# Turning the next batch's tokens by crossbar transfers instead of TensorE, with two V tiles moved between the last contexts

## The reference

```
xn = layernorm(x)
q, k, v = heads(xn @ Wq.T), heads(xn @ Wk.T), heads(xn @ Wv.T)     # 16 heads of 32
q, k = rope(q), rope(k)
s = softmax(causal(q @ k.T / sqrt(32))) @ v, heads joined, @ Wo.T
h = gelu(bitlinear(xn, w_fc))          # 512 -> 2048; bitlinear: layer norm, ternary weights
g = silu(bitlinear(h, w_proj))         # 2048 -> 512
out = x + s * g
```

## Time and profile before

| | us |
|---|---|
| time, median of 3 runs | 1127.14 (1125.05 to 1127.7) |
| the profiled execution's own time | 1127.08 |
| its span in the trace | 1125.4 |
| TensorE busy | 1100.0 (98%) |
| VectorE busy | 843.7 (75%) |
| ScalarE busy | 791.3 (70%) |
| GpSimd busy | 503.7 (45%) |

### The profile page before, as it was taken

How to read it: one execution, slowest core, us unless ns; L and a number is a source line. 1 busy time by engine, 2 the same in 40 slices (tenths; PEclk the granted TensorE clock), 3 DMA queues, 4 the chain that set the end, 5 groups by cost and what they waited for, 6 DMA issues and landing times.

```text
span 1125.4 us, 20210 instructions
## 1 busy us (share of the span) xinstructions
PE 1100.0 (98%) x7548; PEld 609.2 (54%) x7548; DVE 843.7 (75%) x1595; ACT 791.3 (70%) x1510; POOL 503.7 (45%) x915
## 2 busy tenths in 40 slices
PE   4989999999999999999999999999999999999998
PEld 3555654458444574446644475445844467444663
DVE  7987977798558986489756996479865898648964
ACT  4788984589835888269872798448982588826984
POOL 2135361473606635265433745156361663526533
PEclk9999999999999999999999999999999999999999
DMA  9492002920019101381016510193011910136101
GB/s 317 160 106 47 1 3 66 110 79 21 2 39 158 40 2 31 43 127 38 3 29 74 95 38 4 29 105 83 20 7 40 153 38 2 31 47 85 39 16 62
DMA packets 52610, 67.30 MB, mean 60 GB/s; under 512 B 9376, under 2 KB 34336, under 8 KB 52000
## 3 DMA queue, kind: packets, MB, share of 16 engines
q1 hardware_dynamic: 52512, 66.02, 32.3%
HBM read 31.98 MB, written 8.40 MB: 36 GB/s over the span
## 4 chain that ended last, share of the span: by engine, by line
PE 92%; DVE 3%; ACT 2%; POOL 1%; DMA 1%; issue 1%; SPq 0%; DVEq 0%; POOLq 0%
PE banks L433 23%; PE banks L561 20%; PE banks L606 14%; PE banks L687 7%; PE banks L668 7%; PE banks L540 6%; PE banks L450 5%; PE banks L617 4%; PE banks L547 2%; ACT banks L873 2%; PE banks L464 1%; PE banks L404 1%; PE banks L471 1%; DVE mix L1163 1%; DMA v_sb<-in_L_attn_Wv_dram 1%
## 5 line engine op out<-in xcount | busy, mean ns | idle before, releaser
L873 ACT ACTIVATE banks<-banks,mix,scl 128x384 f32<-128x384 f32 (+2 forms) x384 | 248.1, 649 | 21.1 <-POOL mix L1375 15.7
L1163 DVE TENSOR_REDUCE mix<-banks 128x1 f32<-128x512 f32 (+3 forms) x352 | 216.1, 638 | 27.6 <-PE banks L547 23.3
L561 PE MATMUL banks<-xT,fcT 128*128 128x512 f16 x1024 | 229.4, 381 | 3.2 <-ACT xh_buf L837 2.7
L606 PE MATMUL banks<-proj_ones,arena 128*128 128x256 f16 (+1 forms) x1536 | 213.3, 273 | 0.0
L896 ACT ACTIVATE arena<-banks,scl 128x1280 f32<-128x1280 f32 x128 | 162.1, 1329 | 30.8 <-PE banks L668 27.9
L1366 POOL TENSOR_TENSOR xh_buf<-xh_buf 128x512 f32<-128x512 f32 x120 | 152.3, 1269 | 70.4 <-ACT xh_buf L837 69.2
L433 PE MATMUL banks<-xT,qkT 128*128 128x512 f16 x768 | 168.5, 379 | 0.0
L561 PEld LDWEIGHTS banks<-xT,fcT 128*128 128x128 f16 x1024 | 98.8, 98 | 123.1 <-ACT xh_buf L837 6.7
L606 PEld LDWEIGHTS banks<-proj_ones,arena 128*128 128x128 f16 x1536 | 141.7, 97 | 35.8
L1375 POOL TENSOR_SCALAR mix<-mix,scl 128x1 f32<-128x1 f32 (+1 forms) x288 | 76.5, 266 | 174.3 <-DVE mix L1163 172.9
L1135 DVE TENSOR_TENSOR arena<-banks,mix 128x512 f32<-128x512 f32 x128 | 79.5, 684 | 93.9 <-PE banks L433 93.9
(11 more groups left out here) (165 smaller groups left out, 1445.0 us busy)
## 6 DMA issues: line engine op xcount, KB each, us to landing
stacks<-xh_buf SPq DMA_DIRECT2D x96, 128.0 KB, 5.2
stacks<-split_buf SPq DMA_DIRECT2D x96, 128.0 KB, 7.1
out_dram<-arena SPq DMA_DIRECT2D x32, 256.0 KB, 2.0
xr_buf<-in_L_attn_x_dram SPq DMA_DIRECT2D x7, 1024.0 KB, 9.9
resid<-in_L_attn_x_dram SPq DMA_DIRECT2D x28, 256.0 KB, 5.7
stacks<-in_L_ffn_w_fc_dram SPq DMA_DIRECT2D x1, 4096.0 KB, 26.1
arena<-in_L_ffn_w_proj_dram SPq DMA_DIRECT2D x1, 4096.0 KB, 15.1
mix<-norm_row SPq DMA_DIRECT2D x8, 256.0 KB, 5.0
```

Of the source, the lines that this page charges most:

```text
L561: mm = pe.matmul(banks[:, UP_BANKS[f % NUB], :], fcT[:, c, f * P:(f + 1) * P], xT[:, part, c, :], start=(c == 0 and part == 0), stop=(c == ...
L606: mm = pe.matmul(banks[:, DOWN_BANKS[h % 3], 0:cols.stop - cols.start], hid[:, part, f, t * P:(t + 1) * P], proj_ones[:, f, cols], start=( ...
L873: mm = nc.scalar.activation(block, block, ACT.Exp, scale=col(EXP_SCALE), bias=exp_bias[:, i, h0 + k:h0 + k + 1], accum_out=row_sum[:, i, h ...
L1163: nc.vector.tensor_reduce(row_max[:, i, h0:h0 + n], scores_of(r), AX_X, ALU.max).then_inc(max_ready, 1)
```

## The change

From the second batch on, PE no longer turns tokens.

- VectorE normalises a tile in place in `x_sb`, copies it to 16 bits (hi) and subtracts for lo, both into `x_parts` (in `xh_buf`), a tile as 128 tokens x (hi 512, lo 512). It does tiles 0 and 1 where it normalised all four before (`normalise_and_split(b + 1, 0)`), and tiles 2 and 3 behind the context of group 1 and the gate scales.
- SP issues four transposing DMAs, one a tile, from `x_parts` into `xT` (`turn_tokens` on SP), behind `spread_norms` and ahead of the `resid` loads. Each raises its own semaphore `xT_dma[t]`. In batch 1, w_o's load waits for all four.
- PE does V's tiles 0 and 1 of the next batch in the last turn of the context loop, tile 0 ahead of group 3's contexts and tile 1 behind their first part; tiles 2 and 3 start the next body. The four tiles have banks 0 to 3 (before: 0 and 1 by turns). Each waits for its own transfer. QK's first pair waits for ScalarE's copies of V tiles 2 and 3.
- ScalarE has no copies of turned tokens left; before tanh it waits for VectorE's split, and before the first V copy for all contexts.

```diff
+V_AHEAD = 2
+        x_parts = xh_buf[:].rearrange("p a t -> p (a t)").bitcast(F16).rearrange("p (t a d) -> p t a d", t=NT, a=2)
@@ SP
+            def turn_tokens(b):
+                sp.wait_ge(fc_ps, b * FC)
+                for t in range(NT):
+                    sp.wait_ge(tokens_split, (b - 1) * NT + t + 1)
+                    sp.dma_start(xT[:, :, :, t * P:(t + 1) * P].rearrange("p a c n -> p (a c) n"),
+                                 x_parts[:, t].rearrange("p a d -> p (a d)"), transpose=True).then_inc(xT_dma[t], 16)
                     if b == 1:
-                        sp.wait_ge(xT_ps, 2 * NT)
+                        for s in xT_dma:
+                            sp.wait_ge(s, 16)
                         load_weight(raw_attn[3], w_o, 3)
                 if not last:
                     store_norms(b + 1)
                     spread_norms(b + 1)
+                    turn_tokens(b + 1)
@@ PE
+            def v_tile(b, t, first=False):
+                if first:
...
+                else:
+                    if t == 0:
+                        pe.wait_ge(probs_ready, b * H - 1)
+                    if t == NT - 1:
+                        pe.wait_ge(probs_ready, b * H)
+                    pe.wait_ge(xT_dma[t], 16 * b)
+                three_products(banks[:, t % 2 if first else t, :],
+                               lambda a, r, c: (xT[:, a, c, t * P:(t + 1) * P], voT[:, 0, r, c, :]),
+                               ND, "v").then_inc(v_ps, 1)
+                for t in range(0 if first else V_AHEAD, NT):
+                    v_tile(b, t, first)
+                        if pair == 0 and not first:
+                            pe.wait_ge(v_ready, b * NT + 3 + half)
-                        if g == NG and not last:
-                            if k == 0:
-                                for t in range(3):
-                                    turn_tokens(b + 1, t)
-                            if k == 1:
-                                turn_tokens(b + 1, 3)
+                        if g == NG and not last and k < V_AHEAD:
+                            v_tile(b + 1, k)
@@ ACT
+                    if t == 0 and not first:
+                        act.wait_ge(pv_ps, b * NG)
                 if not last:
-                    split_tokens(b + 1)
+                    act.wait_ge(tokens_split, (b + 1) * NT)
@@ DVE
+                def normal(t):
+                    nc.vector.tensor_scalar(x_sb[:, t, :], x_sb[:, t, :], ln[:, 6, t:t + 1], ln[:, 7, t:t + 1],
+                                            ALU.mult, ALU.add).then_inc(tokens_normal, 1)
+                def high(t):
+                    dve.wait_ge(tokens_normal, at + t + 1)
+                    nc.vector.tensor_copy(x_parts[:, t, 0, :], x_sb[:, t, :]).then_inc(tokens_hi, 1)
+                def low(t):
+                    dve.wait_ge(tokens_hi, at + t + 1)
+                    nc.vector.tensor_tensor(x_parts[:, t, 1, :], x_sb[:, t, :], x_parts[:, t, 0, :], ALU.subtract).then_inc(tokens_split, 1)
...
                     if g == 1 and not last:
-                        normalise(b + 1)
+                        normalise_and_split(b + 1, 0)
                     finish_context(g)
                     if g == 2 and not last:
-                        split_tokens(b + 1)
                         rope_rows(b + 1)
                     if g == 1:
...
+                        if not last:
+                            normalise_and_split(b + 1, 2)
```

More of the change, by code:

```diff
@@ L217, in program @@
         xT_ps, xhi_ready, xlo_ready = sem("xT_ps"), sem("xhi_ready"), sem("xlo_ready")
+        tokens_normal, tokens_hi, tokens_split = sem("tokens_normal"), sem("tokens_hi"), sem("tokens_split")
+        xT_dma = [sem(f"xT_dma{t}") for t in range(NT)]
         rope_row_ready = sem("rope_row_ready")
@@ L454, in late_out_projection, with turn_tokens @@
                             yield
[L456 to L462, removed]
+            def turn_tokens(t):
+                pe.wait_ge(xhat_ready, t + 1)
                 for c in range(ND):
@@ L484, in last_out_projection, with body @@
                     last_out_products(b, t, range(1 if t < NT - 1 else 0, NG)).then_inc(wo_ps, 1)
[L486 to L490, removed]
+            def v_tile(b, t, first=False):
+                if first:
+                    pe.wait_ge(xlo_ready, t + 1)
+                    if t == 0:
                         pe.wait_ge(w_kept, ND)
                     if t >= 2:
[L493 to L496, removed]
+                        pe.wait_ge(v_ready, t - 1)
+                else:
+                    if t == 0:
+                        pe.wait_ge(probs_ready, b * H - 1)
[5 more added lines that the diff above has]
+                               ND, "v").then_inc(v_ps, 1)
+            def body(b, first=False, last=False):
+                for t in range(0 if first else V_AHEAD, NT):
+                    v_tile(b, t, first)
                     for u in TURNS_AFTER_V[t] if first else []:
@@ L721, in _ @@
             for t in range(2):
-                turn_tokens(0, t, first=True)
+                turn_tokens(t)
             for t in range(2, NT):
                 turn_weights(t, t + 1)
-                turn_tokens(0, t, first=True)
+                turn_tokens(t)
             spread_largest(1, 0, 4)
@@ L769, in sum_magnitudes, with normalise, split_tokens @@
                                      accum_out=w_part[:, N_ABS * m + k:N_ABS * m + k + 1]).then_inc(w_abs_part, 1)
-            def normalise(b, t):
-                act.wait_ge(ln_ready, b + 1)
+            def normalise(t):
+                act.wait_ge(ln_ready, 1)
                 nc.scalar.activation(xhat[:, t, :], x_sb[:, t, :], ACT.Identity, scale=ln[:, 6, t:t + 1],
                                      bias=ln[:, 7, t:t + 1]).then_inc(xhat_ready, 1)
-            def split_tokens(b, tiles=range(NT)):
+            def split_tokens(tiles):
                 for t in tiles:
-                    act.wait_ge(xT_ps, b * NT + t + 1)
+                    act.wait_ge(xT_ps, t + 1)
                     nc.scalar.copy(xT[:, 0, :, t * P:(t + 1) * P],
@@ L784, in _ @@
             for t in range(NT):
-                normalise(0, t)
+                normalise(t)
             for u in range(2):
                 keep_weights(u)
-            split_tokens(0, (0,))
+            split_tokens((0,))
             for u in range(2, ND):
                 keep_weights(u)
-            split_tokens(0, range(1, NT))
+            split_tokens(range(1, NT))
             def body(b, first=False, last=False):
                 for t in range(NT):
+                    if t == 0 and not first:
+                        act.wait_ge(pv_ps, b * NG)
                     act.wait_ge(v_ps, b * NT + t + 1)
-                    nc.scalar.activation(v_sb[:, t, :], banks[:, t % 2, :], ACT.Copy, scale=norm_c[:, t:t + 1]).then_inc(v_ready, 1)
+                    nc.scalar.activation(v_sb[:, t, :], banks[:, t % 2 if first else t, :], ACT.Copy, scale=norm_c[:, t:t + 1]).then_inc(v_ready, 1)
                     for u in TURNS_AFTER_V[t] if first else []:
@@ L1100, in scale_by_gate, with normalise_and_split, split_tokens @@
                         nc.vector.tensor_tensor(result[:, t, :], result[:, t, :], xhat[:, t, :], ALU.add).then_inc(last_ready, 1)
-            def normalise(b):
-                dve.wait_ge(ln_ready, b + 1)
[L1105 to L1109, removed]
+            def normalise_and_split(b, t0):
+                at = (b - 1) * NT
+                def normal(t):
[7 more added lines that the diff above has]
+                    nc.vector.tensor_tensor(x_parts[:, t, 1, :], x_sb[:, t, :], x_parts[:, t, 0, :], ALU.subtract).then_inc(tokens_split, 1)
+                dve.wait_ge(ln_ready, b + 1)
+                normal(t0)
+                high(t0)
+                normal(t0 + 1)
+                low(t0)
+                high(t0 + 1)
+                low(t0 + 1)
+            def split_tokens(tiles):
                 for t in tiles:
-                    dve.wait_ge(xhi_ready, b * NT + t + 1)
+                    dve.wait_ge(xhi_ready, t + 1)
                     tile = xT[:, :, :, t * P:(t + 1) * P]
```

6 lines of the change are left out of this document (3 added, 3 removed).

## The result

The changed kernel takes 1164.33 us (median of four runs, 1164.05 to 1165.36) against 1127.42 for the one before in the same session: ratio 1.0333, 95% interval 1.0315 to 1.0351. It is slower, by 37 us where 34 were forecast (1164 us against the forecast 1161).

A forecast was written before the change was run, and what follows sets the result against it. The prediction took PE (TensorE), busy 98% of the span, as the bound. From 1127.1 us, -14.4 of transposes, +37.3 of waits and +11.2 of slow clock gave 1161 us; own range 1140 to 1178, 8 in 10 1127 to 1198.

The forecast's parts named there:

- PE is the bound; the transposes are the whole gain: At seven batch boundaries, PE loses 2.05 us of transposes each: 14.4 us off, the whole possible gain.
- V tiles move no total: V tiles 0 and 1 between contexts: same matmuls earlier, 2.60 us a tile, covering masks, no change in total.
- VectorE's split is hidden: VectorE's scale, copy and subtraction, 3.34 us per pair of tiles, finish before SP sends them and cost PE nothing.
- SP comes as PE does, so the whole flight is waited for: First transfer at each boundary: offset -0.20 us in the mean, flight 5.5, so PE waits 5.3 us, 37.3 in seven.
- The clock: Behind each boundary's stall PE's clock falls and loses 1.6 us: 11.2 us in seven, bounds 0 and 3 each.
- w_o's load at nothing: In batch 1 w_o's load waits for all four transfers; cost nothing, about 7 us if transfers land 3.4 us apart.
- A: Rival: same 37.3 us of waits for the first transfers, but PE's clock holds: 1150 us; chance 15%.
- B: Rival: the transfer lands in 2.0 us like the stores, waits sum to 12.6 us: 1128.5 us, no change; chance 12%.
- D: Rival: flight of about 2.2 us or less, so waiting costs under 2.05 us a boundary; 1118 at 1.0 us; chance 9%.
- C: Rival: slow crossbar, tiles 5 us apart, V tile 3 late, w_o's load adds about 7: some 1202 us; chance 14%.
- The 2.6 us: The page's flight for a 256 KB transfer, 2.0 us fixed plus bytes; would give a 2.4 us wait and 1130 us.
- The 10.5 us a tile: The page's 1309 ns per 128x128 block by DMA, eight blocks one after another; an estimate near 1340 us.

The follow-up runs named there:

- run 11: Changed kernel with all four transfers ahead of the norms' stores and broadcast, rope rows formed next batch, w_o loaded in batch 0: 1114.64 us, ratio 0.9895 to the kernel before.
- run 1: Changed kernel with SP's four transfers moved ahead of the norms' broadcast, still behind the small stores: 1138.67 us, ratio 1.0085 to the kernel before.
- run 5: Changed kernel with SP's order stores, wait for their landing, four transfers, then broadcast: 1148.73 us, ratio 1.019 to the kernel before.
- run 3: Changed kernel with 24 extra matmuls on PE ahead of the wait for the first transfer: 1163.43 us, ratio 1.0324 to the kernel before.
- run 8: As run 6 (two transfers, stores, two transfers, broadcast), but all V tiles behind group 3's contexts: 1128.19 us, ratio 1.0006 to the kernel before.
- run 9: As run 6, with rope rows formed at the head of the next batch and w_o loaded in batch 0: 1120.26 us, ratio 0.9941 to the kernel before.
- run 12: As run 9, but all V tiles behind group 3's contexts: 1120.71 us, ratio 0.9946 to the kernel before.
- run 6: Changed kernel with SP's order two transfers, norms' small stores, two transfers, broadcast: 1129.3 us, ratio 1.0018 to the kernel before.
- run 7: Changed kernel with SP's order all four transfers, then the stores, then the broadcast: 1131.52 us, ratio 1.0032 to the kernel before.
- run 2: Changed kernel with all four V tiles behind group 3's contexts, transfers left in place: 1154.24 us, ratio 1.0223 to the kernel before.

## Why the prediction was right, step by step

*PE is the bound; the transposes are the whole gain.* Right, with 1.85 us a boundary for the 2.05 of the rows: run 11, where no boundary has a gap, shows it.

*V tiles move no total.* Right but for 0.1 us a tile (2.70 for 2.60), and "they cover masks" was worth more than the nothing I put on it: 8.2 to 8.4 us of mask waits appear in the three runs with V behind. It was never a term of the sum, since the change has it.

*VectorE's split is hidden.* Right. In run 1 tile 0 was split 6.5 us before PE wanted it, where 6.7 were forecast; that it went at just the predicted 568.2 is luck, since that run's timeline is shifted by its earlier boundaries. A pair takes about 3.8 us and not 3.34, without effect on PE.

*SP comes as PE does, so the whole flight is waited for.* Right. The waits are 33.5 us, forecast 37.3. The term was mis-sized on both sides: the seven first flights are 3.94 to 5.36 us, 4.5 in the mean and not 5.5, and in the mean PE was ready 0.1 us before SP's issue instead of 0.2 after it, with another 0.1 from landing to V's start. The mechanism given, a place behind the broadcast, is shown by the landings, 1.0 to 1.1 us behind the broadcast's at all seven boundaries, and by run 5, where the flight without it is 3.2 us.

*The clock.* Right in kind, shown by run 3. The term was 11.2 us and measured 15.0: where the one stall of 2.72 us cost 1.6, these cost 1.6 to 1.7 at three boundaries and 2.5 at four. The 3.8 us more here and the 3.8 us less of the waits cancel, and that is luck. The one stall that the term was taken from is also less firm than it looked: the same stall stands in batch 0 of every kernel, and behind it the clock fell in nine of the fourteen traces and stayed up in those of runs 1, 3, 8, 9 and 11. In run 11 the first eight matmuls behind it are as fast as the next eight:

```profile
74.80 1.90 PE L584 MATMUL banks<-xT,fcT 128*128 128x512 f16 x8 [2.73 <-ACT xh_buf L857]
76.53 1.04 PE L418 MATMUL banks<-ident,gate_sum 128*128 128x128 f32 x8
77.41 1.89 PE L584 MATMUL banks<-xT,fcT 128*128 128x512 f16 x8
```

With the stalls of 4.2 to 5.9 us at the changed kernel's boundaries the clock fell every time.

*w_o's load at nothing.* Measured 0.9 us. A wait of PE's for this value in batch 1 was listed as a sign of being wrong; it shows, but it is small.

The sum by its terms: forecast -14.4 + 37.3 + 11.2 + 0 = 34.1; the terms measured -13.0 + 33.5 + 15.0 + 0.9 = 36.4, of 37.0. The forecast's own range comes to 1139 to 1179 from its terms, not 1140 to 1178; nothing hangs on it.

The rivals. A (the clock holds) fell with the 0.50 in the first stretch. B asked for flights of 2.0 us, D for 2.2 and less; the shortest in any trace is 3.08, and 3.10 for a first tile with nothing ahead. C (a slow crossbar) fell: tiles 1 to 3 never waited, they land at most 3.0 us apart, and plain copies were slower.

The 2.6 us estimated from the Trainium skill, "DMA: Bandwidth & Descriptors" (section "Anatomy of one DMA — SWDGE (gpsimd) path"), compare with 3.1 to 3.3 us in run 5; the page gives its sum for DMAs that GpSimd issues, and these come from SP. The 10.5 us a tile estimated from the Trainium skill, "VectorE: DVE Perf Modes" (section "The three transpose paths"), by adding up eight blocks compare with this same 3.1 to 3.3, so eight blocks in one transfer do not add up.

The prediction did not see how bad the stores ahead are; it named SP's wait for them, and not that they also hold the queue. It cost nothing there, but the first repair (run 1) missed by it, where it was put down as a rival only.

## What to carry to other kernels

When a transform leaves the bounding engine for a DMA, first ask when the queue that carries it is free, not how long it takes: here a flight of 3.2 us became 4 to 5.4 behind a broadcast and 9.5 behind 512 stores of 4 bytes. Send what the bounding engine waits for ahead of small stores that nobody needs soon, and early enough to have landed when they are issued (a transfer sent 1.4 us ahead of them took 11.8 us at one boundary), then look for who waited for those (VectorE's rope rows here) and move that wait too. And count a stall of the matmul engine with the slow clock that can follow it: 15 us on top of 33.5.

## What the runs showed of the hardware

- 512 stores of 4 bytes from SBUF to DRAM, four DMAs of SP's, keep SP from the broadcast, which waits for their landing, for 8.4 to 13.4 us from the first one's issue (boundaries of the kernel before, the changed one and run 3). Transfers issued behind them in the same queue land late: 9.48 us for one of 3.22 us. So did, at one boundary of runs 8, 9 and 12, one issued 1.4 us ahead of them (11.6 to 11.8 us). In the chain of run 5 the last of the stores alone is 9.40 us.
- A transposing DMA of 256 KB within SBUF takes SP about 1.3 us to issue and lands after 3.1 to 3.4 us with nothing ahead in its queue (first tiles of runs 5 to 9, 11 and 12; 3.7 to 4.7 at the seventh boundary of all of these but 5 and 7). A plain copy in 256-byte pieces at the same place behind the broadcast landed later than the transposing one at all seven boundaries, 5.5 us after issue in the mean against 4.5.
- A wait's length does not decide alone whether the clock falls. In run 2 it fell behind all seven waits, down to 2.28 us; in run 5 waits of 2.10, 2.52 and 2.57 us left it up; the stall of 2.72 us in batch 0, with the same work around it, did the one and the other. In run 9 a wait of 3.05 us left it at full speed, as these rows show (the V tile, then the stretch with PEclk 1.00):

```profile
442.74 2.76 PE L448 MATMUL banks<-voT,xT 128*128 128x512 f16 x12 [3.05 <-DMA xT<-xh_buf]
...
442.00:446.00 4.00, 3.26 (x20) 1.38 (x24) 0.00 (x0) 0.00 (x0) 0.00 (x0) 1.00 0.62 65
```
